# Order of the weights' split and of the first key loads in a transformer-like block

## What is computed

```python
x = x + attn(_layernorm(x, axis=-1), w_project, w_out)
# attn:
qkv = jnp.einsum('bsd,od->bso', x, w_project)          # 2048 x 1536
q, k, v = ...                                          # 16 heads of 32
att = jnp.einsum('bhqd,bhkd->bhqk', q, k) / math.sqrt(HEAD_DIM)
att = softmax(where(causal, -1e9, att))
out = jnp.einsum('bhqk,bhkd->bhqd', att, v)
return jnp.einsum('bsd,od->bso', out, w_out)
```

## Time and profile before

| what | value |
|---|---|
| median of 3 runs | 3377.06 us (3371.04 to 3385.72) |
| profiled execution, own time | 3374.1 us |
| its span, first to last instruction | 3372.4 us |
| mean granted TensorE clock | 0.958 |
| TensorE busy | 3143.9 us, 93% of the span |
| VectorE busy | 2083.4 us, 62% |
| ScalarE busy | 1592.0 us, 47% |
| GpSimd busy | 904.2 us, 27% |
| projections | 0 to about 164 us |
| attention's first load | issued at 165.27 us |

### The profile page before, as it was taken

The page is one execution under the profiler, slowest core; times in us unless marked ns, Lnnn a source line. Parts: engine busy times, 40 slices in busy tenths (PEclk is TensorE's granted clock), DMA queues, the critical chain, the costliest instruction groups (busy, mean ns, idle before and its releaser), DMA issues. The chain is left out here.

```text
span 3372.4 us, 62799 instructions
## 1 busy us (share of the span) xinstructions
PE 3143.9 (93%) x15962; PEld 2452.9 (73%) x15965; DVE 2083.4 (62%) x3584; ACT 1592.0 (47%) x2095; POOL 904.2 (27%) x772
## 2 busy tenths in 40 slices
PE   7989999999799899999999968878998999999996
PEld 6745555555577699999899933335787999999996
DVE  4266666663585466666666649987654666666664
ACT  2224444444321256665556656634123656656663
POOL 0011000110111233333333314432012444443332
PEclk9969999999899999999999978988998999999998
DMA  5331111130310367776776540114115777777664
GB/s 178 114 72 39 39 40 39 40 101 1 118 32 22 109 168 174 177 169 168 170 180 166 116 134 0 50 63 147 40 40 155 178 180 183 170 181 168 176 138 111
DMA packets 141339, 383.49 MB, mean 114 GB/s; under 512 B 22112, under 2 KB 22880, under 8 KB 137568
## 3 DMA queue, kind: packets, MB, share of 16 engines
q1 hardware_dynamic: 87456, 252.66, 23.7%
q0 software_dynamic: 52608, 127.69, 20.3%
q10 hardware_dynamic: 1152, 1.57, 0.2%
HBM read 281.42 MB, written 104.63 MB: 114 GB/s over the span
## 5 line engine op out<-in xcount | busy, mean ns | idle before, releaser
L1728 DVE TENSOR_TENSOR first_lo<-first_raw,first_hi x232 | 562.7, 2426 | 121.3 <-ACT first_hi L1671 121.3
L1625 POOL DMA_INDIRECT acc_rows<-g_y,first_ids_out x232 | 377.3, 1626 | 902.2 <-ACT g_y L1682 712.1
L594 DVE TENSOR_REDUCE b_part_max<-b_p_ring 128x1 f32<-128x512 f32 (+3 forms) x640 | 359.9, 606 | 229.3 <-PE b_p_ring L681 142.1
L1671 ACT ACTIVATE first_hi<-first_raw x232 | 469.6, 2024 | 48.3 <-DMA first_raw<-in_expert_weights_dram 33.1
L568 ACT ACTIVATE b_probs<-b_p_cols 128x1024 f32<-128x1024 f32 (+1 forms) x320 | 269.3, 893 | 320.9 <-PE b_p_cols L699 320.9
L1721 DVE TENSOR_TENSOR g_hidden<-g_gate,g_p_up 128x352 f32<-128x352 f32 x232 | 120.9, 521 | 446.8 <-PE g_p_up L1788 446.4
L1786 PE MATMUL g_p_gate<-first_hi,g_rows_hi 128*128 x928 | 321.8, 347 | 6.5 <-DVE first_lo L1728 6.5
L1682 ACT ACTIVATE g_y<-g_p_y,first_rows_in 128x512 f32<-128x512 f32 x232 | 159.6, 688 | 329.6 <-PE g_p_y L1804 329.5
L1787 PE MATMUL g_p_gate<-first_lo,g_rows_hi 128*128 x928 | 303.0, 327 | 0.0
L1788 PE MATMUL g_p_gate<-first_hi,g_rows_lo 128*128 x928 | 301.6, 325 | 0.0
L1786 PE MATMUL g_p_up<-first_hi,g_rows_hi 128*128 x928 | 297.9, 321 | 0.0
(11 more groups left out here) (326 smaller groups left out, 6479.1 us busy)
## 6 DMA issues: line engine op xcount, KB each, us to landing
first_raw<-in_expert_weights_dram SPq DMA_DIRECT2D x248, 544.0 KB
acc_rows<-f_acc SPq DMA_DIRECT2D x34, 256.0 KB, 2.0
qk_hi<-a_hi SPq DMA_DIRECT2D x32, 256.0 KB, 2.6
qk_lo<-a_lo SPq DMA_DIRECT2D x32, 256.0 KB, 2.9
xn_rows<-f_xn SPq DMA_DIRECT2D x8, 1024.0 KB, 5.2
b_q_stack<-qk_hi SPq DMA_DIRECT2D x28, 256.0 KB
b_k_stack<-qk_hi SPq DMA_DIRECT2D x28, 256.0 KB
first_raw<-in_expert_weights_dram SPq DMA_DIRECT2D x2, 2176.0 KB, 8.8
```

The source lines that it names most:

```text
L594: v.tensor_reduce(part_max[:, h, t % BT, c:c + 1], p_ring[:, ring, 0:w], AX.X, ALU.max).then_inc(rows_free, 1)
L1625: pool.indirect_dma_start(out=acc_rows, out_offset=bass.IndirectOffsetOnAxis(ap=ids_out[:, i:i + 1].bitcast(U32), axis=0), in_=y[:, n, :], ...
L1671: act.activation(hi[:, bass.ds(place, PIECE)], raw[:, bass.ds(source, PIECE)], ACT.Copy).then_inc(split_hi_ready, 1)
L1728: v.tensor_tensor(lo[:, bass.ds(place, PIECE)], raw[:, bass.ds(source, PIECE)], hi[:, bass.ds(place, PIECE)].bitcast(F32), ALU.subtract).t ...
```

## The change

In the first block of the projections, ScalarE and VectorE split the first part of the weights before the rows' pieces; VectorE makes the second part's low half right behind the rows, then the low parts of products 0 and 1, and only then normalizes block 1 (ScalarE's root moves with it); the third part's low half comes before the low part of product 4. TensorE's product 0 waits for the low part of the rows quarter by quarter. In attention, ScalarE's queue issues the first keys of blocks 0 and 1 alone, SP's queue takes those of blocks 2 and 3, each behind the queries of its block; the three parts of keys are loaded in the order 1, 2, 0.

```diff
--- before.py
+++ after.py
@@ scalar, stage_qkv
                 norm.scalar_root(act, 0)
+                high_weights(0)
                 for c in range(KD):
                     high_rows(0, c)
-                for i in range(3):
+                for i in range(1, 3):
                     high_weights(i)
                 for b in range(NB):
-                    if b + 1 < NB:
+                    if b >= 1 and b + 1 < NB:
                         norm.scalar_root(act, b + 1)
                     for i in range(PER):
+                        if b == 0 and i == TURN_AT - 2:
+                            norm.scalar_root(act, 1)
                         n = b * PER + i
@@ vector, stage_qkv
                 normalize(0)
+                low_weights(0)
                 for c in range(KD):
                     low_rows(0, c)
-                low_weights(0)
+                low_weights(1)
                 for b in range(NB):
-                    if b + 1 < NB:
+                    if b >= 1 and b + 1 < NB:
                         normalize(b + 1)
-                    if b == 0:
-                        low_weights(1)
-                        low_weights(2)
                     for i in range(PER):
+                        if b == 0 and i == TURN_AT - 2:
+                            normalize(1)
+                        if b == 0 and i == TURN_AT:
+                            low_weights(2)
                         if i < NQK:
@@ tensor, stage_qkv
                 for b in range(NB):
-                    pe.wait_ge(xT_lo_ready, (b + 1) * KD)
+                    if b >= 1:
+                        pe.wait_ge(xT_lo_ready, (b + 1) * KD)
...
                         for p, (c, xs, ws) in enumerate(parts):
+                            if n == 0 and p % 3 == 0:
+                                pe.wait_ge(xT_lo_ready, c + 1)
@@ load_first, stage_attention
-                for part in range(3):
+                for part in (0, 1, 2) if offset == 0 else (1, 2, 0):
@@ sync, stage_attention
                         for j in range(NB):
                             load_first(sp, q_stack[0], 0, j)
+                            if j >= 2:
+                                load_first(sp, k_stack[0], D, j)
@@ scalar, stage_attention
-                for j in range(NB):
+                for j in range(2):
                     load_first(act, k_stack[0], D, j)
```

## The result

| | before | changed |
|---|---|---|
| median, 19 runs each | 3373.14 us | 3364.33 us |
| lowest to highest | 3363.75 to 3389.25 | 3358.22 to 3375.33 |
| profiled execution: span | 3372.4 us | 3360.0 us |

The ratio is 0.9974, 95% interval 0.9963 to 0.9985: the change brings 8.8 us (5.1 to 12.5). The time alone does not tell the forecast from its nearest rival, the transfers (9.0 less); it does exclude the three others (2.3 and 3.1 less, 1.9 more). What tells them apart stands in the traces.

The account below looks back on a forecast made before the run. TensorE was taken as busy nearly throughout, so time returns only where it idles or runs at its lower clock. Terms -9.4 + 1.3 = -8.1 us took the median from 3377.06 to 3369.0 us, range 3362 to 3379.

Parts of the forecast that it names:

- the transfers: Rival, attention's first loads: transfers, not issues, set the landing; SP 0 to 0.8 us later, 3368.1 us; chance 0.20.
- the three others: Rivals: backlog stays and clock rises late (0.20), 3374.8; slower than before (0.05), 3379.0; second stall stays (0.05), 3374.0 us.
- The first third ahead: Projections' start: weights' first third split before the rows' pieces, so the first product starts at 15.15, 4.4 us earlier.
- the sign of being wrong: Projections: the turn of block 1 later than 34 us in the profile after would show the forecast wrong.
- Waits by quarter: Product 0: none of four waits stops TensorE; waiting for all four would start it 1.5 us later, at 16.6.
- The second stall: Fifth product: TensorE's 3.58 us idle goes; block 1's normalizing is late next; sixth product 9.4 us earlier, at least 7.5.
- the lower clock: First product: matmuls at 0.44 us until the step to 0.23 after 4.8 us; it takes 5.05 us, to 20.2.
- A store: Projections: stores issued behind block 1's row loads; the first buffer they free is wanted by ScalarE at 31.2, TensorE at 41.
- The first keys: Attention's start: SP issues 36 loads instead of 24 and goes on 1.3 us later, bounds 0.8 to 5.2.
- The one of a slow queue: Rival, attention's first loads: one queue gets only 127 GB/s, landing 9.4 us later, kernel 3379.0 us; chance 0.05.
- The second stall stays: Rival, projections: low weights or buffers still come late; 4.4 us back less 1.3, 3374.0 us; chance 0.05.
- The sum: Whole kernel: 9.4 us won in the projections, 1.3 lost at the first keys, 8.1 us less in all.

Follow-up runs that it names:

- e5: Kernel before with only the weights' first third ahead of the rows and waits by quarter, block 1 normalized where it was; median 3370.42 us, ratio 0.999 to before.
- e4: Changed kernel with product 0 waiting for all four pieces of rows at once; median 3364.91 us, ratio 0.9986 to the kernel before.
- e3: Changed kernel with all 24 first key loads back on ScalarE's queue, new order of parts kept; median 3367.00 us, ratio 0.9975 to the kernel before.
- e10: Changed kernel with all 24 first key loads on SP's queue, which then issues 48 loads; median 3368.86 us, ratio 0.9986 to the kernel before.
- e6: Changed kernel with the first pair's shifts moved through DRAM before the second pair's stacks; median 3352.75 us, ratio 0.9930 to the kernel before.
- e7: Changed kernel with block 1's rows loaded before the weights' third part and normalized behind the second low weights, third high part later; 3358.15 us, ratio 0.9958 to before.
- e2: Kernel before with only attention's part of the change, projections as before; median 3368.30 us, ratio 0.9993 to the kernel before.
- e1: Changed kernel with attention's first loads as before, so the projections' part alone; median 3359.81 us, ratio 0.9962 to the kernel before.
- e8: Changed kernel with keys on ScalarE's queue, shifts before the second pair's stacks and block 1's rows early; 3353.27 us, ratio 0.9935 to the kernel before.
- e11: Changed kernel with shifts before the second pair's stacks and block 1's rows early, keys split between queues; 3350.42 us, ratio 0.9923 to the kernel before.

## Why the prediction was right

- **The first third ahead.** Forecast: product 0 4.4 us earlier. e5, whose first rows were taken up as early as before (3.69 for 3.67 us), shows 15.18 against 15.15 forecast. In the changed kernel's trace all of the first loads came later, and it was 16.88. For the same reason the turn of block 1 (33.60) came close to the sign of being wrong, later than 34: that sign was counted from the start and not from the landing.
- **Waits by quarter.** Forecast: none of them stops TensorE, and waiting for all four costs 1.5 us at product 0 but mostly not behind it. The changed kernel has no such wait. e4: a wait of 1.41, and 1.0 at the turn, within the 0 to 1.2 expected of e4 and not nothing.
- **The second stall.** Forecast: gone, with the rows of block 1 as what is late next, 9.4 us in all. Measured from those rows' landing, 9.4 (140.12 to 140.21 before, 130.75 after; also 130.76 in e3 and e10, 130.75 in e6). The forecast put the turn 6.39 us behind the statistics' start (31.45 - 25.06); it was 6.35. e7 confirms what is late next.
- **One term was off.** The first product was to run at the lower clock for 4.8 us, as before. The step between matmuls fell to 0.25 us already at 18.73, 1.85 us after the first. The turns at 15.26 run straight into the product now, where before 4.92 us of idle time lay between. In the nine traces without a wait there it took 1.29 to 3.57 us, in the three with one (before, e2, e4) 3.96 to 4.82. It changed nothing, since the turn waits for the rows.
- **A store came later than I let it.** ScalarE's fifth copy was to find its buffer free near 31.2; it waited 3.1 us for the store, to 34.65. Nobody needed it before the ninth product.
- **The first keys.** Forecast 1.3 us later, 0.8 to 5.2 as bounds. Measured from load to step 18.43, 18.55 (e4), 18.63 (e7) and 18.84 against 17.42, 17.40, 17.59 and 18.12 with 24 loads: means 18.6 and 17.6, 1.0 us. The issue-bound step that I assumed (36 issues and 2.5 us, 18.7) holds; e10 shows it at 48. The rival of the transfers (0 to 0.8 us) falls, since SP goes on 2.2 to 2.3 us after its last issue; the 1.0 alone would be close to it. The one of a slow queue falls too.
- **A rival was priced wrong.** "The second stall stays" was to bring back 4.4 us less 1.3. e5 has that stall and brings back nothing in the projections (140.76 for 140.21), so the rival's change would be 1.3 us slower and not 3.1 faster.
- **The sum.** -9.4 + 1.3 = -8.1 forecast, -9.4 + 1.0 = -8.4 by the marks in the traces, -8.8 (-12.5 to -5.1) measured. That the runs come within 0.7 us of the forecast is in part luck, since their interval reaches 3.7 us to either side; it is the marks in the traces that bear out the terms.
- **What the one pair of traces shows beyond it.** Its spans differ by 12.4 us, 7.3 at attention's first load, 6.1 at the scores, 9.0 at the end of the pairs. Some of the difference within the pairs is one fall of the clock, in the section below; what lies behind attention has no edit in it, and its cause stays open.

## What to carry to other kernels

Before a wait is taken away, ask what the engine would wait for next: here one edit won 4.4 us at the first product and nothing at the fifth, and only with the new order of VectorE's work did the change bring 9.4. When small loads are moved to another queue, multiply their number by the issue time of that queue and compare it with the landing of the last: here the transfers were the bound at 24 loads, the issues at 36. And a short write on which other engines wait does not belong behind large loads on the same queue; moving it ahead brought 10.5 us in the traces, more than the whole change.

## What the runs showed of the hardware

**The clock falls after short waits, sometimes.** In e1 TensorE waited once in the projections,

```profile
PE a_p_turn L308 <- DVE a_x L141: 2.3, 1, 2.3
```

and the clock of the stretch behind it was 0.89 on average:

```profile
34.00:50.00 16.00, 16.00 (x71) 13.03 (x70) 10.32 (x19) 4.95 (x9) 0.00 (x0) 0.89 0.63 202
```

That is 71 matmuls in 16 us; the changed kernel, after a wait of 1.95 us, has 79 at full clock:

```profile
34.00:50.00 16.00, 16.00 (x79) 13.27 (x78) 10.84 (x20) 5.56 (x10) 0.00 (x0) 1.00 0.65 218
```

The turn stands 6.35 us behind the rows' landing in both, so the wait itself costs e1 nothing more. The slower matmuls behind it cost 1.6 us (132.33 from the landing to attention's first load, for 130.75). The same happens between pairs of heads in attention, in the kernel before:

```profile
445.00:450.00 5.00, 5.00 (x20) 3.31 (x20) 3.46 (x8) 2.35 (x6) 1.37 (x4) 0.50 0.35 93
```

and not in the changed one, where the scores start 6.1 us earlier:

```profile
440.00:445.00 5.00, 4.84 (x24) 2.80 (x24) 3.71 (x8) 1.13 (x4) 1.75 (x3) 1.00 0.99 220
```

The length of the wait does not decide it alone. TensorE's idle time just before is shorter in the kernel before, where the clock falls (1.65 us), than at the same place in the changed one (2.05 us, before the matmul at 435.60):

```profile
442.81 0.72 PE L681 MATMUL b_p_ring<-b_k_stack,b_q_stack 96*128 96x512 f32 x2 [1.65 <-issue]
```

Of the other traces, e1, e3, e5, e8 and e11 have such a fall to about half in the same place, some 230 us behind the first scores, e7 a smaller one, e10 one only at a later pair; e1 and e5 have another at that later pair; e2, e4 and e6 have none. So it does not follow the edits of the projections or of the shifts, and what decides it stays open. From the first to the last start of the scores it took 598.8 to 599.6 us in the four traces with no fall at any pair (the changed kernel, e2, e4, e6) and 601.3 to 606.0 in the others: 2 to 7 us of a single trace, which is why the terms above are read between marks inside a stage and not from spans.

**Loads at the start of the program** landed up to 2.2 us later in one execution than in another (25.06 to 27.25 for block 1's rows in kernels that load in the same order), and the stage behind them moves along; why they do stays open.
